# Diagonal attention: the turned query rows stand once, half of the heads in each row group, in place of all heads in both

## The chip, the cores and the metric

The kernel runs on one core of a Trainium2 chip. The metric is device time in microseconds, the median of the runs shown.

## The reference, cut to what matters

Four blocks follow one another on a residual of 2 x 2048 tokens of 128 channels: a hybrid block (state space, time crystal, wavelet attention, mixture of experts), an FFN-like attention, the diagonal attention, and the FFN-like attention again. The change touches the third only:

```python
Q = (X_embed @ W_q + b_q) * scale      # K likewise, V without scale
Q, K, V = (t.reshape(n, heads, l, d) for t in (Q, K, V))   # heads 16, d 8
scores = jnp.einsum('neax,nebx->neab', Q, K)
A = jax.nn.softmax(scores, axis=2)     # over the queries a
diag = jnp.diagonal(A, axis1=2, axis2=3)
out = (diag[..., None] * V).reshape(n, l, hid)
return out @ W_o + b_o
```

The reshape has no transposition, so a "head" e of the reference is a block of 128 tokens, and its 2048 rows are 128 tokens times 16 slices of 8 channels. The kernel calls the slices heads. For each tile of 128 tokens it needs, for every key (128 tokens x 16 slices), the maximum and the sum of exponentials over all 2048 queries of the same tile. The order of the queries does not matter for either.

## The kernel before, in words

`phase_F` handles 32 tiles, one after another. For each, the projections are split into three bfloat16 parts, and the products of parts that matter stand as 64 rows (8 terms x 8 channels) per head: POOL spreads them token by token into `d_q_rows` and `d_k_rows` (L2471, L2478). TensorE turns them (L2289), and the copies into `d_qT` and `d_kT` (L2366 on VectorE, L2426 on ScalarE) leave 64 rows for each head, once in partitions 0 to 63 and once in 64 to 127, the two row groups of TensorE. There are four groups of 16 transposes for a tile: group 0 and 1 are the queries of heads 0 to 7 and 8 to 15, group 2 and 3 the keys. In each, all eight heads are turned into both row groups.

A tile has 32 steps, two for each key head: step n takes key head n // 2 and the query half n % 2. Its score is two matmuls side by side, one in each row group (L2304), into two of six PSUM banks; VectorE takes the maximum of the 1024 columns (L2372), ScalarE the exponentials with their sum (L2434, whose accumulator is read by an instruction of its own). The six banks are a ring of three steps: score n waits for the exponential of n - 3.

The order of the side work is written out by hand with generators. `beside` runs, after each of the 32 scores of tile t, one piece of the preparation of tile t + 1 and one piece of the closing of tile t - 1, on each of TensorE, VectorE and ScalarE. TensorE projects the next tile after score 0 (L2277), turns the output of the last tile after score 10 and multiplies it by the output weights after score 12 (L2312, L2316), and turns rows from score 14 on. VectorE copies group 0 after its reduction 16, ScalarE the groups 1, 2 and 3 after its exponentials 18, 20 and 22. POOL does the spreading and small arithmetic in one line: close tile t - 1, prepare tile t + 1. SyncE has only the loads ahead of the stage.

All side outputs of TensorE share the two remaining banks. The list `side` gives their order (projection, turned output, output, rows 0 to 3), and `pe_side` lets a unit wait until the one two places before it has been read: rows 2 for VectorE's copy of rows 0, rows 3 for ScalarE's copy of rows 1. In TensorE's order the wait for the spread query rows stands at step 14, that for the key rows ahead of group 2, at step 18. The stage's first tile is prepared with nothing beside it.

Lines that the steps touch: L2274 to L2294 `pe_prep`, L2246 `pe_side`, L2296 `pe_score`, L2319 `beside`, L2343 the wait for the last copy ahead of score 0, L2349 `dve_prep`, L2416 `act_prep`, L2429 `act_score`, and the wait on `turned` in `pool_prep`. The same two-row-group matmul stands in the FFN-like attention at L1872: `k2[half, w, h, f, :]` streams from the same columns of both halves.

Of the kernel before, what the change touches and what calls it, by code (L numbers as in the profile page):

```python
# [11 lines left out]
P = 128  # L12
D = 128
BANK = 512
# [85 lines left out]
def build(nc, a, out, shape, phases=("M", "T", "C", "D", "E", "F", "E2")):  # L100
# [5 lines left out]
    with ctx:  # L106
# [16 lines left out]
        def sb(stack, name, shp, dt=F32):  # L123
            return stack.enter_context(nc.sbuf_tensor(name, shp, dt))
# [2054 lines left out]
        def phase_F():  # L2179
# [7 lines left out]
            with ExitStack() as st:  # L2187
# [7 lines left out]
                part = sb(st, "d_parts", [P, 3, 2 * HID], BF16)  # L2195
                uq = sb(st, "d_q_rows", [P, 2, NH, len(TERMS), HD], BF16)
                uk = sb(st, "d_k_rows", [P, 2, NH, len(TERMS), HD], BF16)
                qT = sb(st, "d_qT", [2 * ROWS, 2, NH * P], BF16)
                kT = sb(st, "d_kT", [2 * ROWS, 2, NH * P], BF16)
                dg = sb(st, "d_diag", [P, 3, NH])  # L2200
                dj = sb(st, "d_diag_terms", [P, HID])
# [13 lines left out]
                biased = signal("diag_biased", tl)  # L2215
                q_spread = signal("diag_q_spread", tl)
                k_spread = signal("diag_k_spread", tl)
                turned = signal("diag_rows_turned", [(t, k) for t in tl for k in range(4)])
                row_dve = signal("diag_rows_dve", tl)
                row_act = signal("diag_rows_act", [(t, k) for t in tl for k in range(1, 4)])  # L2220
                scored = signal("diag_scored", range(R * STEPS))
                maxed = signal("diag_max", range(R * STEPS))
                summed = signal("diag_exp", range(R * STEPS))
# [12 lines left out]
                for t in range(-1, R + 1):  # L2236
                    if t + 1 < R:
                        side.append(("qkv", t + 1))
                    if 0 <= t - 1 < R:
                        side += [("turn", t - 1), ("out", t - 1)]  # L2240
                    if t + 1 < R:
                        side += [("rows", t + 1, k) for k in range(4)]
                side_at = {u: n for n, u in enumerate(side)}
                side_bank = lambda *u: side_at[u] % 2

# [26 lines left out]
                    leave(SP)  # L2272

                def pe_prep(t):  # L2274
                    b, i, s = t // NT, t % NT, t % 2
                    bk = pe_side("qkv", t)
                    T.matmul(bank(bk)[:, 0:3 * HID], chans[:, b, PAD + i * P:PAD + (i + 1) * P], w[:, :],  # L2277
                             start=True, stop=True).then_inc(*projected.up(t))
                    for _ in range(14):
                        yield  # L2280
                    T.wait_ge(*q_spread(t))
                    for k in range(4):
                        u = uk if k >= 2 else uq
                        if k == 2:
                            T.wait_ge(*k_spread(t))
                        rows = bank(pe_side("rows", t, k)).bitcast(BF16)
                        for q in range(8):
                            for r in range(2):
                                last = T.transpose(rows[ROWS * r:ROWS * r + ROWS, q * P:(q + 1) * P],  # L2289
                                                   u[:, s, 8 * (k % 2) + q].rearrange("p n x -> p (n x)"), identb[:, :])  # L2290
                            if q == 7:
                                last.then_inc(*turned.up(t, k))
                            if q % 3 == 2:
                                yield  # L2294

                def pe_score(t, n):  # L2296
                    s, jb, hf = t % 2, n // 2, n % 2
                    at = t * STEPS + n
                    if at >= 3:
                        T.wait_ge(*summed(at - 3))  # L2300
                    for jj in range(2):
                        c = 2 * hf + jj
                        half = slice(ROWS * jj, ROWS * jj + ROWS)
                        last = T.matmul(bank(2 + 2 * (at % 3) + jj), kT[half, s, jb * P:(jb + 1) * P], qT[half, s, c * BANK:(c + 1) * BANK],  # L2304
                                        start=True, stop=True)
                    last.then_inc(*scored.up(at))

# [22 lines left out]
                def pe():  # L2330
                    enter(T)
                    for b in range(NB):
                        T.wait_ge(*ln_out("F", b))
                        for g in range(4):
                            pe_turn_group("F", b, g, 4 * b + g, norm)
                    leave(T)
                    enter(T)
                    for _ in pe_prep(0):
                        pass

                    def score(t, n):
                        if n == 0:
                            T.wait_ge(*row_act(t, 3))  # L2343
                            T.wait_ge(*row_dve(t))
                        pe_score(t, n)
                    beside(pe_prep, pe_close, score)
                    leave(T)

                def dve_prep(t):  # L2349
                    s = t % 2  # L2350
                    bk = side_bank("qkv", t)
                    yield
                    V.wait_ge(*projected(t))
                    if t >= 1:
                        V.wait_ge(*k_spread(t - 1))
                    if t >= 3:
                        V.wait_ge(*closed(t - 3))
                    V.tensor_tensor(qf[:, s, :], bank(bk)[:, 0:2 * HID], bias[:, 0:2, :].rearrange("p n h -> p (n h)"), ALU.add)
                    V.tensor_tensor(vf[:, t % 3, :], bank(bk)[:, 2 * HID:3 * HID], bias[:, 2, :], ALU.add).then_inc(*biased.up(t))
                    for _ in range(15):  # L2360
                        yield
                    V.wait_ge(*turned(t, 0))
                    if t >= 2:
                        V.wait_ge(*scored((t - 1) * STEPS - 1))
                    rows = bank(side_bank("rows", t, 0)).bitcast(BF16)
                    V.tensor_copy(qT[:, s, 0:8 * P], rows).then_inc(*row_dve.up(t))  # L2366
                    yield

                def dve_score(t, n):
# [45 lines left out]

                def act_prep(t):  # L2416
                    s = t % 2
                    for k in range(1, 4):
                        for _ in range(18 if k == 1 else 2):
                            yield  # L2420
                        A.wait_ge(*turned(t, k))
                        if t >= 2:
                            A.wait_ge(*scored((t - 1) * STEPS - 1))
                        dst = kT if k >= 2 else qT
                        rows = bank(side_bank("rows", t, k)).bitcast(BF16)
                        A.copy(dst[:, s, (k % 2) * 8 * P:(k % 2 + 1) * 8 * P], rows).then_inc(*row_act.up(t, k))  # L2426
                    yield

                def act_score(t, n):  # L2429
# [29 lines left out]
                def pool_prep(t):  # L2459
                    s = t % 2  # L2460
                    heads = lambda x: x.rearrange("p (h o x) -> p h o x", o=1, x=HD)
                    G.wait_ge(*biased(t))
                    gstep(G.tensor_copy(part[:, 0, :], qf[:, s, :]))
                    gstep(G.tensor_tensor(rest[:, :], qf[:, s, :], part[:, 0, :], ALU.subtract))
                    gstep(G.tensor_copy(part[:, 1, :], rest[:, :]))
                    gstep(G.tensor_tensor(part[:, 2, :], rest[:, :], part[:, 1, :], ALU.subtract))
                    if t >= 2:
                        G.wait_ge(*turned(t - 2, 3))
                    for g in range(3):
                        rows = uq[:, s, :, of_q[g], :]  # L2470
                        last = G.tensor_copy(rows, wide(heads(part[:, g, 0:HID]), 2, rows.shape[2]))  # L2471
                        if g < 2:
                            gstep(last)
                    last.then_inc(*q_spread.up(t))
                    G.wait_ge(*q_spread(t))
                    for g in range(3):
                        rows = uk[:, s, :, of_k[g], :]
                        last = G.tensor_copy(rows, wide(heads(part[:, g, HID:2 * HID]), 2, rows.shape[2]))  # L2478
                        if g < 2:
                            gstep(last)  # L2480
                    last.then_inc(*k_spread.up(t))
                    G.wait_ge(*k_spread(t))
                    gstep(G.tensor_tensor(dj[:, :], qf[:, s, 0:HID], qf[:, s, HID:2 * HID], ALU.mult))
                    d4 = dj[:, :].rearrange("p (h x) -> p h x", x=HD)
                    gstep(G.tensor_tensor(d4[:, :, 0:4], d4[:, :, 0:4], d4[:, :, 4:8], ALU.add))
                    gstep(G.tensor_tensor(d4[:, :, 0:2], d4[:, :, 0:2], d4[:, :, 2:4], ALU.add))
                    gstep(G.tensor_tensor(dg[:, t % 3, :], d4[:, :, 0], d4[:, :, 1], ALU.add))
# [70 lines left out]
```

## Time and profile before

| | |
|---|---|
| median of 3 runs | 4824.35 us (4823.6 to 4824.75) |
| the profiled execution, its own time | 4827.53 us |
| its span | 4826.2 us |
| granted TensorE clock, mean | 0.801 |
| busy share of the span | TensorE 78%, VectorE 72%, ScalarE 61%, POOL 17% |
| the diagonal attention's tiles | 2693.4 us to about 4020 us of the span |

The span is counted from the first to the last instruction. In the page's chain of work that ended last, the reduction L2372 is the largest line with 11% and the exponential L2434 has 4%. Busy shares over the span average stages with different limits, so the stretches of the one stage are read below.

### The profile page before, as it was taken

What the parts mean: (1) busy time and instruction counts of PE and PEld (TensorE: products, weight loads), DVE (VectorE), ACT (ScalarE), POOL (GpSimd) and SP (SyncE); (2) the same over time, 40 slices, a digit from 0 to 9 for tenths busy, and PEclk for the clock granted to TensorE, in tenths of its full rate; (3) what the DMA queues carried; (4) which work ended last, traced back from release to release, by engine and by line L of the source; (5) the groups of instructions that cost most, each with busy time, mean ns of one, the idle gap of its engine ahead of it and who ended that gap; (6) DMA issues with size and microseconds to landing.
All of it is one profiled execution on the core that took longest, in us unless ns stands there. A gap on an engine that the chain in (4) does not pass through costs nothing.

```text
span 4826.2 us, 78862 instructions
## 1 busy us (share of the span) xinstructions
PE 3784.1 (78%) x31382; PEld 2009.6 (42%) x31382; DVE 3457.4 (72%) x5239; ACT 2956.7 (61%) x4913; POOL 838.6 (17%) x1094
## 2 busy tenths in 40 slices
PE   6888558858869996899999566666666664899998
PEld 4666333222234442567666211111111111567666
DVE  6888666476451003778787899999999996778787
ACT  3444126626623333566665699999999995566665
POOL 2444210000036762000000111111111110000000
PEclk8999759969979998999999555555555556999999
DMA  1000000000022210000000000000000000000000
GB/s 42 1 1 1 1 3 1 1 0 1 1 72 36 44 26 17 8 15 2 11 2 5 2 1 1 1 1 1 1 1 1 1 1 18 8 15 2 11 2 19
DMA packets 49884, 45.20 MB, mean 9 GB/s; under 512 B 21203, under 2 KB 34910, under 8 KB 49502
## 3 DMA queue, kind: packets, MB, share of 16 engines
q1 hardware_dynamic: 49518, 40.16, 4.0%
q8 instruction: 250, 4.10, 0.4%
q14 instruction: 116, 0.95, 0.1%
HBM read 29.52 MB, written 2.23 MB: 7 GB/s over the span
## 4 chain that ended last, share of the span: by engine, by line
PE 47%; DVE 29%; issue 11%; ACT 10%; POOL 2%; DMA 1%; SPq 1%; DVEq 0%; ACTq 0%; POOLq 0%
DVE d_negmax L2372 11%; PE psum L1872 7%; PE psum L1901 6%; PE psum L1887 5%; DVE f_m_E L2017 5%; PE psum L1507 5%; PE psum L1530 4%; ACT d_junk L2434 4%; PE psum L1124 2%; PE psum L1113 2%; PE psum L1098 2%; ACT wl_p L1345 2%; DVE f_pT_E L2036 1%; DVE wl_negmax L1250 1%; PE psum L498 1%
## 5 line engine op out<-in xcount | busy, mean ns | idle before, releaser
L2372 DVE TENSOR_REDUCE d_negmax<-psum 128x1 f32<-128x1024 f32 x1024 | 1184.6, 1215 | 101.4 <-PE psum L2304 101.4
L2434 ACT ACTIVATE d_junk<-psum,d_negmax 128x1024 bf16<-128x1024 f32 x1024 | 1137.8, 1128 | 75.7 <-DVE d_negmax L2372 68.0
L2304 PE MATMUL psum<-d_qT,d_kT 64*128 64x512 bf16 x2048 | 605.5, 600 | 440.6 <-ACT d_junk L2434 424.2
L2123 ACT ACTIVATE hidden<-psum,f_nm_E 128x1024 f32<-128x1024 f32 x512 | 566.5, 1113 | 141.7 <-DVE f_nm_E L2020 141.5
L2017 DVE TENSOR_REDUCE f_m_E<-psum 128x1 f32<-128x1024 f32 x512 | 602.3, 1218 | 47.7 <-PE psum L1872 47.5
L1872 PE MATMUL psum<-f_k_E,f_q_swapped_E 64*128 64x512 f32 x1024 | 526.9, 624 | 6.6 <-ACT hidden L2123 6.6
L1872 PE MATMUL psum<-f_k_E,f_q_E 64*128 64x512 f32 x1024 | 526.9, 624 | 2.8 <-DMA f_q_swapped_E<-f_q_E 1.4
L1901 PE MATMUL psum<-f_pT_E,f_v_E 128*64 128x128 f32 x8192 | 503.7, 276 | 2.5 <-DVE residual L2047 2.5
L2130 ACT COPY f_pT_E<-psum 128x512 f32<-128x512 f32 x512 | 300.1, 586 | 319.8 <-PE psum L1887 319.7
L2036 DVE COPY f_pT_E<-psum 128x512 f32<-128x512 f32 x512 | 351.7, 687 | 157.4 <-PE psum L1887 146.9
L2304 PEld LDWEIGHTS psum<-d_qT,d_kT 64*128 64x128 bf16 x2048 | 106.0, 101 | 857.9 <-ACT d_junk L2434 805.5
L1901 PEld LDWEIGHTS psum<-f_pT_E,f_v_E 128*64 128x64 f32 x8192 | 442.5, 137 | 20.1 <-ACT f_pT_E L2130 2.8
L1887 PEld LDWEIGHTS psum<-ident,hidden 64*128 64x128 f32 x8192 | 317.4, 140 | 234.8 <-issue 185.3
L1664 POOL TENSOR_TENSOR moe_h<-moe_h,moe_gates_on_all 128x512 f32<-128x512 f32 x256 | 322.8, 1294 | 494.2 <-DMA moe_gates_on_all<-moe_gate_spill 364.6
L1250 DVE TENSOR_REDUCE wl_negmax<-psum 128x1 f32<-128x1024 f32 x256 | 305.5, 1222 | 142.4 <-PE psum L1098 138.4
L1887 PE MATMUL psum<-ident,hidden 64*128 64x64 f32 x8192 | 358.6, 227 | 47.8 <-DVE f_pT_E L2036 44.8
L1649 ACT ACTIVATE moe_h<-psum,moe_b 128x512 f32<-128x512 f32 x256 | 175.4, 687 | 271.8 <-PE psum L1530 271.8
L1345 ACT ACTIVATE wl_p<-psum 128x1024 f32<-128x1024 f32 x256 | 253.2, 1026 | 110.8 <-PE psum L1113 110.4
L1507 PE MATMUL psum<-moe_h,moe_w 128*128 128x512 f32 x512 | 232.2, 597 | 8.9 <-POOL moe_h L1664 8.9
L1530 PE MATMUL psum<-normed_channels,moe_w 128*128 128x512 f32 x512 | 235.4, 604 | 0.0
L1594 DVE COPY moe_yT<-psum 128x512 f32<-128x512 f32 x8 | 5.5, 692 | 312.3 <-PE psum L1507 312.3
L2434 ACT ACTIVATION_READ_ACCUMULATOR d_junk<-psum,d_negmax 128x1 f32 x1024 | 216.6, 212 | 0.0
(313 smaller groups left out, 5246.5 us busy)
## 6 DMA issues: line engine op xcount, KB each, us to landing
moe_gates_on_all<-moe_gate_spill SPq DMA_DIRECT2D x8, 2048.0 KB, 15.8
f_q_swapped_E<-f_q_E SPq DMA_DIRECT2D x64, 128.0 KB, 2.4
moe_w<-in_moe_w SPq DMA_DIRECT2D x8, 256.0 KB, 4.0
out<-residual SPq DMA_DIRECT2D x1, 2048.0 KB, 8.7
residual<-in_hidden_states SPq DMA_DIRECT2D x2, 768.0 KB, 7.4
residual<-in_hidden_states SPq DMA_DIRECT2D x2, 256.0 KB, 3.4
m_taps<-in_m_conv SPq DMA_DIRECT2D x4, 128.0 KB
level_sums<-in_c_sums SPq DMA_DIRECT2D x1, 512.0 KB
```

The source lines that it names most:

```text
L1250: V.tensor_reduce(negm[:, i, h:h + 1], two(slot(*step)), X, ALU.max, negate=True).then_inc(*maxed.up(b, h, i))
L1507: last = T.matmul(acc, w2[:, e * FT + f, :], hbuf[:, n % 2, f, :], start=False, stop=(e == E_ - 1 and f == FT - 1))
L1530: T.matmul(bank(f), w1[:, e, f * P:(f + 1) * P], chans[:, b, PAD + g * BANK:PAD + (g + 1) * BANK], start=True, stop=True).then_inc(*made.u ...
L1872: last = T.matmul(bank(2 * f + jj), (q if jj == h else q_sw)[half, w, qs], k2[half, w, h, f, :], start=True, stop=True)
L1887: last = T.transpose(bank(4 + r)[:, q * 64:(q + 1) * 64], pb[half, u % 2, kt * P:(kt + 1) * P], ident[half, half])
L1901: last = T.matmul(bank(6)[64 * h:64 * h + 64, 0:P], vt[:, n % 2, kt, h, :], pT[:, (2 * t + h) % 4, kt, :], start=(kt == 0), stop=(kt == NT ...
L2017: last = V.tensor_reduce(m2[:, u % 4, f:f + 1], two(2 * f), X, ALU.max)
L2036: V.tensor_copy(pT[:, u % 4, 8 * g:8 * g + 8, 64:P], bank(5).rearrange("p (q n) -> p q n", n=64)).then_inc(*pT_dve.up(u, g))
L2123: A.activation(pb[:, u % 2, f * 2 * BANK:(f + 1) * 2 * BANK], two(2 * f), ACT.Exp, bias=nm[:, u % 4:u % 4 + 1], scale=SC, accum_out=rs[:, ...
L2304: last = T.matmul(bank(2 + 2 * (at % 3) + jj), kT[half, s, jb * P:(jb + 1) * P], qT[half, s, c * BANK:(c + 1) * BANK], start=True, stop=True)
L2372: V.tensor_reduce(mh[:, t % 2, n // 2, n % 2:n % 2 + 1], two(2 + 2 * (at % 3)), X, ALU.max, negate=True).then_inc(*maxed.up(at))
L2434: A.activation(junk[:, at % 3, :], two(2 + 2 * (at % 3)), ACT.Exp, bias=mh[:, t % 2, n // 2, n % 2:n % 2 + 1], accum_out=sh[:, t % 2, n // ...
```

## The change

The query rows are turned in one group in place of two. That group puts heads 0 to 7 into the first row group and heads 8 to 15 into the second. `d_qT` has half the columns. A step's two matmuls now take the same columns of `d_qT`, which are different heads in the two halves. The keys stay twice and are groups 1 and 2 now, copied by ScalarE after its exponentials 18 and 20.

```diff
--- before.py
+++ after.py
@@ -2195,7 +2195,7 @@
                 part = sb(st, "d_parts", [P, 3, 2 * HID], BF16)
                 uq = sb(st, "d_q_rows", [P, 2, NH, len(TERMS), HD], BF16)
                 uk = sb(st, "d_k_rows", [P, 2, NH, len(TERMS), HD], BF16)
-                qT = sb(st, "d_qT", [2 * ROWS, 2, NH * P], BF16)
+                qT = sb(st, "d_qT", [2 * ROWS, 2, NH * P // 2], BF16)
                 kT = sb(st, "d_kT", [2 * ROWS, 2, NH * P], BF16)
                 dg = sb(st, "d_diag", [P, 3, NH])
                 dj = sb(st, "d_diag_terms", [P, HID])
@@ -2215,9 +2215,9 @@
                 biased = signal("diag_biased", tl)
                 q_spread = signal("diag_q_spread", tl)
                 k_spread = signal("diag_k_spread", tl)
-                turned = signal("diag_rows_turned", [(t, k) for t in tl for k in range(4)])
+                turned = signal("diag_rows_turned", [(t, k) for t in tl for k in range(3)])
                 row_dve = signal("diag_rows_dve", tl)
-                row_act = signal("diag_rows_act", [(t, k) for t in tl for k in range(1, 4)])
+                row_act = signal("diag_rows_act", [(t, k) for t in tl for k in range(1, 3)])
                 scored = signal("diag_scored", range(R * STEPS))
                 maxed = signal("diag_max", range(R * STEPS))
                 summed = signal("diag_exp", range(R * STEPS))
@@ -2239,7 +2239,7 @@
                     if 0 <= t - 1 < R:
                         side += [("turn", t - 1), ("out", t - 1)]
                     if t + 1 < R:
-                        side += [("rows", t + 1, k) for k in range(4)]
+                        side += [("rows", t + 1, k) for k in range(3)]
                 side_at = {u: n for n, u in enumerate(side)}
                 side_bank = lambda *u: side_at[u] % 2
 
@@ -2272,6 +2272,7 @@
                     leave(SP)
 
                 def pe_prep(t):
                     b, i, s = t // NT, t % NT, t % 2
                     bk = pe_side("qkv", t)
                     T.matmul(bank(bk)[:, 0:3 * HID], chans[:, b, PAD + i * P:PAD + (i + 1) * P], w[:, :],
@@ -2279,15 +2280,16 @@
                     for _ in range(14):
                         yield
                     T.wait_ge(*q_spread(t))
-                    for k in range(4):
-                        u = uk if k >= 2 else uq
-                        if k == 2:
+                    for k in range(3):
+                        u = uk if k else uq
+                        if k == 1:
                             T.wait_ge(*k_spread(t))
                         rows = bank(pe_side("rows", t, k)).bitcast(BF16)
                         for q in range(8):
                             for r in range(2):
+                                eighth = 8 * (k - 1 if k else r) + q
                                 last = T.transpose(rows[ROWS * r:ROWS * r + ROWS, q * P:(q + 1) * P],
-                                                   u[:, s, 8 * (k % 2) + q].rearrange("p n x -> p (n x)"), identb[:, :])
+                                                   u[:, s, eighth].rearrange("p n x -> p (n x)"), identb[:, :])
                             if q == 7:
                                 last.then_inc(*turned.up(t, k))
                             if q % 3 == 2:
@@ -2299,9 +2301,8 @@
                     if at >= 3:
                         T.wait_ge(*summed(at - 3))
                     for jj in range(2):
-                        c = 2 * hf + jj
                         half = slice(ROWS * jj, ROWS * jj + ROWS)
-                        last = T.matmul(bank(2 + 2 * (at % 3) + jj), kT[half, s, jb * P:(jb + 1) * P], qT[half, s, c * BANK:(c + 1) * BANK],
+                        last = T.matmul(bank(2 + 2 * (at % 3) + jj), kT[half, s, jb * P:(jb + 1) * P], qT[half, s, hf * BANK:(hf + 1) * BANK],
                                         start=True, stop=True)
                     last.then_inc(*scored.up(at))
 
@@ -2340,7 +2341,7 @@
 
                     def score(t, n):
                         if n == 0:
-                            T.wait_ge(*row_act(t, 3))
+                            T.wait_ge(*row_act(t, 2))
                             T.wait_ge(*row_dve(t))
                         pe_score(t, n)
                     beside(pe_prep, pe_close, score)
@@ -2363,7 +2364,7 @@
                     if t >= 2:
                         V.wait_ge(*scored((t - 1) * STEPS - 1))
                     rows = bank(side_bank("rows", t, 0)).bitcast(BF16)
-                    V.tensor_copy(qT[:, s, 0:8 * P], rows).then_inc(*row_dve.up(t))
+                    V.tensor_copy(qT[:, s, :], rows).then_inc(*row_dve.up(t))
                     yield
 
                 def dve_score(t, n):
@@ -2415,15 +2416,14 @@
 
                 def act_prep(t):
                     s = t % 2
-                    for k in range(1, 4):
+                    for k in range(1, 3):
                         for _ in range(18 if k == 1 else 2):
                             yield
                         A.wait_ge(*turned(t, k))
                         if t >= 2:
                             A.wait_ge(*scored((t - 1) * STEPS - 1))
-                        dst = kT if k >= 2 else qT
                         rows = bank(side_bank("rows", t, k)).bitcast(BF16)
-                        A.copy(dst[:, s, (k % 2) * 8 * P:(k % 2 + 1) * 8 * P], rows).then_inc(*row_act.up(t, k))
+                        A.copy(kT[:, s, (k - 1) * 8 * P:k * 8 * P], rows).then_inc(*row_act.up(t, k))
                     yield
 
                 def act_score(t, n):
@@ -2465,7 +2465,7 @@
                     gstep(G.tensor_copy(part[:, 1, :], rest[:, :]))
                     gstep(G.tensor_tensor(part[:, 2, :], rest[:, :], part[:, 1, :], ALU.subtract))
                     if t >= 2:
-                        G.wait_ge(*turned(t - 2, 3))
+                        G.wait_ge(*turned(t - 2, 2))
                     for g in range(3):
                         rows = uq[:, s, :, of_q[g], :]
                         last = G.tensor_copy(rows, wide(heads(part[:, g, 0:HID]), 2, rows.shape[2]))
```

## Rows read from the trace of the kernel before

**Rows 1.** Busy time of two tiles: us, then PE, PEld, DVE, ACT, POOL; PEclk, DMA

```profile
2970.10:3011.61 41.51, 26.00 (x136) 7.63 (x138) 38.37 (x39) 39.08 (x70) 7.97 (x21) 0.54 0.00 1
3011.61:3053.12 41.51, 26.36 (x137) 7.64 (x139) 38.38 (x40) 39.10 (x70) 7.98 (x21) 0.50 0.00 1
```

**Rows 2.** Groups of instructions of the whole stage: busy us, mean ns | idle before

```profile
L2372 DVE TENSOR_REDUCE d_negmax<-psum 128x1 f32<-128x1024 f32 x1024 | 1184.6, 1215 | 101.4 <-PE psum L2304 101.4
L2434 ACT ACTIVATE d_junk<-psum,d_negmax 128x1024 bf16<-128x1024 f32 x1024 | 1137.8, 1128 | 75.7 <-DVE d_negmax L2372 68.0
```

**Rows 3.** VectorE's order of time over one tile: start us, us, what

```profile
3000.62 1.22 DVE L2372 TENSOR_REDUCE d_negmax<-psum 128x1 f32<-128x1024 f32 x1 [0.30 <-PE psum L2304]
...
3005.95 4.61 DVE L2372 TENSOR_REDUCE d_negmax<-psum 128x1 f32<-128x1024 f32 x4
3011.61 3.49 DVE L2372 TENSOR_REDUCE d_negmax<-psum 128x1 f32<-128x1024 f32 x3 [1.05 <-PE psum L2304]
3015.36 2.36 DVE L2372 TENSOR_REDUCE d_negmax<-psum 128x1 f32<-128x1024 f32 x2 [0.27 <-PE psum L2304]
3018.47 8.01 DVE L2372 TENSOR_REDUCE d_negmax<-psum 128x1 f32<-128x1024 f32 x7 [0.75 <-PE psum L2304]
3027.25 1.23 DVE L2372 TENSOR_REDUCE d_negmax<-psum 128x1 f32<-128x1024 f32 x1 [0.77 <-PE psum L2304]
```

**Rows 4.** ScalarE's order of time, from the end of exponential 18

```profile
3009.35 0.19 ACT L2434 ACTIVATION_READ_ACCUMULATOR d_junk<-psum,d_negmax 128x1 f32 x1
3009.44 1.00 ACT L2426 COPY d_qT<-psum 128x1024 bf16<-128x1024 bf16 x1
3010.33 1.13 ACT L2434 ACTIVATE d_junk<-psum,d_negmax 128x1024 bf16<-128x1024 f32 x1
3011.34 0.21 ACT L2434 ACTIVATION_READ_ACCUMULATOR d_junk<-psum,d_negmax 128x1 f32 x1
...
3012.52 1.03 ACT L2426 COPY d_kT<-psum 128x1024 bf16<-128x1024 bf16 x1
3013.41 1.15 ACT L2434 ACTIVATE d_junk<-psum,d_negmax 128x1024 bf16<-128x1024 f32 x1
3014.42 0.23 ACT L2434 ACTIVATION_READ_ACCUMULATOR d_junk<-psum,d_negmax 128x1 f32 x1
...
3016.50 1.18 ACT L2434 ACTIVATE d_junk<-psum,d_negmax 128x1024 bf16<-128x1024 f32 x1
3017.51 0.26 ACT L2434 ACTIVATION_READ_ACCUMULATOR d_junk<-psum,d_negmax 128x1 f32 x1
```

**Rows 5.** TensorE's order of time at score 21

```profile
3010.49 0.53 PE L2289 MATMUL psum<-ident_bf,d_k_rows 128*64 128x128 bf16 x6 [1.07 <-ACT d_qT L2426]
3010.96 0.61 PE L2304 MATMUL psum<-d_qT,d_kT 64*128 64x512 bf16 x2
```

**Rows 6.** Groups of the stage: the transposes of key and query rows

```profile
L2289 PE MATMUL psum<-ident_bf,d_k_rows 128*64 128x128 bf16 x992 | 90.1, 307 | 35.1 <-ACT d_qT L2426 35.1
L2289 PE MATMUL psum<-ident_bf,d_q_rows 128*64 128x128 bf16 x992 | 85.7, 314 | 0.0
```

**Rows 7.** Order of time: TensorE's step 16; POOL's key rows one tile later

```profile
3003.68 0.75 PE L2289 MATMUL psum<-ident_bf,d_q_rows 128*64 128x128 bf16 x10
...
3040.91 1.55 POOL L2478 COPY d_k_rows<-d_parts 128x384 bf16<-128x384 bf16 x3
```

**Rows 8.** Order of time: the first preparation

```profile
2688.12 1.54 POOL L2478 COPY d_k_rows<-d_parts 128x384 bf16<-128x384 bf16 x3
...
2692.32 1.01 ACT L2426 COPY d_kT<-psum 128x1024 bf16<-128x1024 bf16 x1
...
2693.39 0.61 PE L2304 MATMUL psum<-d_qT,d_kT 64*128 64x512 bf16 x2 [1.11 <-ACT d_kT L2426]
```

**Rows 9.** Groups of a stretch of the second FFN attention, its score matmuls

```profile
L1872 PE MATMUL psum<-f_k_E,f_q_swapped_E 64*128 64x512 f32 x416 | 213.0, 623 | 0.0
L1872 PE MATMUL psum<-f_k_E,f_q_E 64*128 64x512 f32 x416 | 212.9, 622 | 0.0
```

## The prediction

> **What bounds the kernel now.** I looked first at the busy time by stretch. One tile of the diagonal attention takes 41.51 us, ScalarE is busy 39.08 and VectorE 38.37 of it; TensorE has room, and its granted clock is 0.50 to 0.54, so nearly all of the stage runs at 1.2 GHz [rows 1]. Then the groups of the stage: VectorE idles 101.4 us, all of it waiting for score matmuls, and ScalarE 68.0 us, waiting for VectorE's maxima [rows 2]. Neither is full, so a cycle holds them. Score n may not start before the exponential of n-3 has freed its two banks, and a reduction needs its score, an exponential its reduction. Third, VectorE's order of time shows where the idle time of a tile sits: back-to-back reductions start every 1.13 us ((8.01 - 1.22) / 6), and one tile has waits of 1.05, 0.27, 0.75, 0.77 and 0.30 us [rows 3]. The three beginning with 1.05, together 2.07, lie at scores 21, 24 and 26, behind the three ScalarE copies of turned rows at steps 18, 20 and 22 [rows 4]. Last, TensorE's order of time: score 21 starts at 3010.96 only because transposes of the fourth group stand ahead of it, and they waited 1.07 us for ScalarE's copy to free a side bank [rows 5]; over the stage it is 35.1 us in 992 / 32 = 31 tiles, all those that prepare a successor [rows 6].
>
> **The change part by part, per prepared tile.**
> Removed on TensorE: 16 of 64 transposes, 0.53 us per six, so about 1.4 us of busy time [rows 5]. TensorE waits for others between scores, so by itself this is worth nothing; the wait in front of them counts below. The first group now turns different heads in its two row groups instead of one head twice; query and key transposes cost 314 and 307 ns now [rows 6], so I take no difference.
> Removed on ScalarE: the copy at step 18 or, seen from the end, the third one. Between exponentials it takes 3010.33 - 3009.44 = 0.89 us of ScalarE's order [rows 4]. VectorE's copy of the first group keeps its shape and place.
> Scores: same count, shapes and banks, only the query columns differ. Maximum and sum run over 1024 other queries of the same 2048; cost nothing.
> Moved: key groups come two steps earlier in TensorE's order, and so does the wait for the spread key rows, from step 18 to step 16. Score 17, and with it VectorE and ScalarE, queue behind it. POOL ends those rows at 3040.91 + 1.55 - 41.51 = 3000.95 of the shown tile; step 16's transposes start at 3003.68 [rows 7]. The cover is 2.7 us; without it the excess would be paid in full. The second key group waits for VectorE's copy at step 18, as the third group does now, without idling. The next projection, the turn and the output find their banks free long before. No DMA moves.
>
> **The sum, by replaying the tile from reduction 17.** Three constants: pace 1.13 us; from the end of an accumulator read to the reduction three steps on, 0.70 us (3014.42 + 0.23 = 3014.65 to 3015.36; 3017.51 + 0.26 = 3017.77 to 3018.47); exponential slot 1.10 us, copy slot 0.89 [rows 3, 4]. Times from here are 3000 plus. Reductions 17 to 20 stay: 5.95, 7.08, 8.21, 9.34. Without the bank wait, 21 starts at the pace, 10.47 (the exponential of 18 ended at 9.54, plus 0.70 = 10.24). Exponentials 19 and 20 stay at 10.33 and 11.43, the last copy is at 12.52, 21 and 22 stay at 13.41 and 14.51, and 23 comes at 15.61 in place of 16.50. So reduction 22 waits for exponential 19: 11.34 + 0.21 + 0.70 = 12.25 (a wait of 0.65); 23 at 13.38; 24 waits for exponential 21: 15.35 (a wait of 0.84); 25 at 16.48; 26 at 17.61, with exponential 23 ended at 16.85 and so no wait. Before, 26 started at 18.47: **0.86 us saved**. ScalarE's own chain says the same, one slot of 0.89 less before exponential 26. From there VectorE runs at its pace, and the waits at the projection (0.77) and at the output (0.30) repeat, since what makes them stands in TensorE's own order. So 2.07 of idle time becomes about 1.2 to 1.5: of the 1.05 removed, most of what follows is late next because the ring has only three places.
>
> 31 tiles x 0.86 = 26.7 us. In the first preparation, where nothing covers it, the third copy and its transposes go, but the first key group must wait for POOL until 2688.12 + 1.54 = 2689.66. The bounds are zero (that wait eats it all) and one whole copy, 1.01, the one that ended just before the score at 2693.39 [rows 8]; I take the middle, 0.5, as neither end has a row for it. Sum 27.2. The profiled execution took 4827.53 with a span of 4826.2, and would take 4800.3; the median of the runs shown is 3.2 below it, 4824.35, which gives **4797.2 us**.
>
> Where no row decides, bounds. Per tile the gain lies between half of the above, 0.43 (the ring waits at 22 and 24 hand on more than I let them), and 1.05 (only the wait goes, nothing grows): 4810.5 to 4791.3. I take 0.86, since both the VectorE replay and ScalarE's chain give it.
>
> **Two rules weighed.** ScalarE is the busier engine by 0.71 us per tile [rows 1], and a rule that looked at occupancy alone would stop the gain there, where VectorE becomes the fuller: 31 x 0.71 + 0.5 = 22.5, or 4801.8. The Trainium skill, Perfetto Trace Analysis, Identifying the Most-Contended Engine, ranks engines in just that way and would have the fullest worked on first. The trace speaks against a floor there, since VectorE still idles 3.14 us per tile and is not full either way.
> A tile with clock 0.54 and one with 0.50 both take 41.51 us [rows 1], so a lower clock here costs nothing that a row shows, down to the 1.2 GHz at which nearly all of it runs already. The Trainium skill, TensorE: Matmul & The Clock Gate, HAM oscillation, says that TensorE left idle gets the lower clock, which speaks against taking transposes away; by it the sum stays as it is.
>
> **The rivals.**
> A, the copies become hidden: with two in place of three the ring absorbs them, all of 2.07 goes, and VectorE sets the time: 4824.35 - 31 x 2.07 - 0.5 = 4759.7. For it: VectorE would still be busy 38.4 of 39.4. Against: each copy delays the score three steps on by 0.89, and the ring's slack is 3 x 1.13 less one round of about 3.15 (0.70 + 1.22 + 1.21 + handover), some 0.24 us. 5%.
> B, no measurable change: the saved slot comes back in front of reductions 22, 24 and the projection, or the heads' new order adds a wait that balances it; under 0.3 us per tile remains, 4815 to 4824. For it: waits in this loop are handed on. Against: from 3009.35 to 3017.51 each operation of ScalarE starts as the one before it ends, so a slot taken out there must show [rows 4]. Also here: the text does not do what it says and a fourth group is still turned; the diff's loops leave no place for one. 7%.
> C, slower: the two score matmuls of a pair now read the same query columns in both row groups, where before they read different ones. If these reads had to take turns, the second 512 columns would come behind the first. 512 columns at 1.2 GHz are 0.43 us beside the 0.61 of a pair now [rows 1, 5]; four waits per tile grow by that, 1.72, and a round of 3.58 exceeds three paces by 0.19, 32 / 3 x 0.19 = 2.0. Less 0.86, that is 2.9 per tile, 32 x 2.9 = 92: 4916. It decides from about 0.22 us on (four waits alone then eat 0.86). Against: in the FFN attention two 64-row matmuls read their moving operand, the key tile, at equal columns in both halves, and both groups show the same busy time, 213 us, side by side [rows 9]. 3%.
>
> **How the numbers follow.** The forecast with its bounds has 85%, A 5%, B 7%, C 3%. About 0.2%, 9.6 us, is what a measurement of this kernel can tell from no change; the weak end of the forecast, 4810.5, still lies beyond it, B mostly does not. The range 4790 to 4810 takes in the bounds and leaves out A, B and C, 15%, and a little at the edges. Faster by over 0.2%: 0.90; within: 0.07; slower: 0.03.
>
> **What would show it.** In VectorE's order of time the period should be 40.6 to 40.7 us; no wait at score 21; waits of about 0.6 at 22 and 0.8 at 24; none at 26; 0.77 and 0.30 unchanged. ScalarE should show 64 copies in place of 96 and the wait of key transposes for a ScalarE copy should be gone. POOL's key rows should end over 2 us before the first key transposes. Wrong would be: score matmuls longer than 0.61 a pair (C), a projection or output wait that has grown (B), or a tile near 39.5 (A).

## The result and the profile after

The changed kernel takes 4795.72 us, the median of 4 runs (4794.66 to 4796.81), against 4823.98 us of the kernel before in the same comparison. The ratio is 0.9943, with a 95% interval of 0.9925 to 0.9960: faster by 0.6%. The forecast was 4797.2 in 4790 to 4810. The profiled execution has a span of 4795.5 us, 30.7 less than before. One of the ten executions of run e2 below took 8661.88 us, for a cause that nothing on record shows, and is left out of its ratio; the median of that run is 4822.6 with or without it.

First the two tiles that answer to [rows 1]. Columns as there: the stretch and its us, busy time of PE, PEld, DVE, ACT and POOL, then PEclk.

```profile
2975.71:3016.36 40.65, 23.82 (x119) 6.68 (x117) 38.28 (x39) 38.24 (x69) 7.93 (x21) 0.58 0.00 1
3016.36:3057.01 40.65, 24.91 (x119) 6.87 (x117) 38.28 (x40) 38.23 (x69) 7.94 (x21) 0.54 0.00 1
```

A tile takes 40.65 us in place of 41.51. ScalarE's busy time fell by 0.85 and VectorE's by 0.1, and the two engines are now equally full, 38.2 and 38.3 us. Neither is full: VectorE still waits 2.37 us in each tile for score matmuls. The granted clock of these two tiles is 0.58 and 0.54, not lower than before.

VectorE's order of time over one tile, which answers to [rows 3]:

```profile
2990.59 1.23 DVE L2373 TENSOR_REDUCE d_negmax<-psum 128x1 f32<-128x1024 f32 x1 [0.30 <-PE psum L2305]
...
2995.33 0.68 DVE L2367 COPY d_qT<-psum 128x1024 bf16<-128x1024 bf16 x1
2995.93 5.74 DVE L2373 TENSOR_REDUCE d_negmax<-psum 128x1 f32<-128x1024 f32 x5
3002.22 2.36 DVE L2373 TENSOR_REDUCE d_negmax<-psum 128x1 f32<-128x1024 f32 x2 [0.56 <-PE psum L2305]
3005.33 10.28 DVE L2373 TENSOR_REDUCE d_negmax<-psum 128x1 f32<-128x1024 f32 x9 [0.75 <-PE psum L2305]
3016.36 1.23 DVE L2373 TENSOR_REDUCE d_negmax<-psum 128x1 f32<-128x1024 f32 x1 [0.76 <-PE psum L2305]
```

The reader should compare starts. Reductions 17 to 21 now run as one piece of five (they were four and a stop of 1.05). Reduction 22 starts at 3002.22, 24 at 3005.33, and from 24 on nine run without a stop. The waits of 0.76 (the next tile's projection) and 0.30 (the output matmul) are where they were. The sum of waits in a tile went from 3.14 to 0.56 + 0.75 + 0.76 + 0.30 = 2.37. That is 0.77 of the 0.86; the rest is in the overlap at each stop (a reduction lasts 1.22 us but follows the last one after 1.13, and a stop hides 0.09 of its length in the end of the instruction before it, so three stops lose more than two).

The groups of the stage, in answer to [rows 2, 6]:

```profile
L2373 DVE TENSOR_REDUCE d_negmax<-psum 128x1 f32<-128x1024 f32 x1024 | 1181.8, 1216 | 77.0 <-PE psum L2305 77.0
...
L2291 PE MATMUL psum<-ident_bf,d_k_rows 128*64 128x128 bf16 x1024 | 86.5, 311 | 0.5 <-POOL d_k_rows L2478 0.5
L2426 ACT COPY d_kT<-psum 128x1024 bf16<-128x1024 bf16 x64 | 64.8, 1014 | 12.0 <-PE psum L2291 12.0
```

ScalarE makes 64 key copies, where it made 96 copies of rows; no ScalarE copy of query rows is left. The key transposes no longer wait for ScalarE, where 35.1 us stood; the 0.5 us for POOL are those of the first preparation, where nothing covers it. VectorE's idle time for scores is 77.0 us, against 101.4.

The first preparation, in answer to [rows 8]:

```profile
2684.64 1.54 POOL L2478 COPY d_k_rows<-d_parts 128x384 bf16<-128x384 bf16 x3
...
2687.41 1.93 ACT L2426 COPY d_kT<-psum 128x1024 bf16<-128x1024 bf16 x2 [12.03 <-PE psum L2291]
...
2689.39 0.61 PE L2305 MATMUL psum<-d_qT,d_kT 64*128 64x512 bf16 x2 [1.25 <-ACT d_kT L2426]
```

From POOL's key rows to the first score it is 2689.39 - 2684.64 = 4.75 us, before 2693.39 - 2688.12 = 5.27: 0.52 saved.

**The account of the span.** From the first score to the end of the last tile's maxima (the VectorE minimum after it) the stage took 4018.49 - 2693.39 = 1325.10 us before and 3987.79 - 2689.39 = 1298.40 now: 26.70 less. The preparation gives 0.52. What follows the stage is 807.71 us in both. The remaining 3.5 us lie ahead of the stage, in code that did not change. They come from the wavelet attention: its reductions L1250 start from 685.3 to 1270.9 us before and from 687.3 to 1267.5 now. They begin 2.0 us later and lie 5.4 us closer together, which is 3.4 us gained. Its stretch in busy times and clock, before and then now:

```profile
687.00:1271.00 584.00, 468.51 (x2663) 167.03 (x2660) 376.37 (x464) 321.72 (x349) 8.90 (x7) 0.85 0.00 1
```

```profile
687.00:1268.00 581.00, 461.74 (x2667) 162.82 (x2665) 378.31 (x465) 322.10 (x349) 8.89 (x7) 0.87 0.00 1
```

The mean clock is 0.85 against 0.87 in the same code. I take this for scatter of the two profiled executions and not for the change: in the eight runs below, none of which changes this code, the same reductions take between 581.9 and 583.7 us from first to last, against 585.6 before and 580.2 after. The medians differ by 28.3 us, nearer to the 27.2 that the stage and its preparation give.

### The profile page after: what moved, and what is told of

It reads as the page before. It is cut to its first block, busy times and chain, and to the rows that moved or that the text cites. A ratio compares the mean times of both kernels' runs of the same rounds, so it can differ in the third digit from the quotient of the medians.

```text
span 4795.5 us, 77776 instructions
## 1 busy us (share of the span) xinstructions
PE 3740.9 (78%) x30870; PEld 1980.5 (41%) x30870; DVE 3451.2 (72%) x5239; ACT 2927.5 (61%) x4881; POOL 837.1 (17%) x1094
## 4 chain that ended last, share of the span: by engine, by line
PE 47%; DVE 29%; issue 11%; ACT 9%; POOL 2%; DMA 1%; SPq 1%; DVEq 0%; POOLq 0%; ACTq 0%
DVE d_negmax L2373 11%; PE psum L1872 7%; PE psum L1901 6%; PE psum L1887 5%; DVE f_m_E L2017 5%; PE psum L1507 5%; PE psum L1530 4%; ACT d_junk L2434 4%; PE psum L1124 2%; PE psum L1113 2%; ACT wl_p L1345 2%; DVE wl_negmax L1250 2%; PE psum L1098 2%; DVE f_pT_E L2036 1%; PE psum L498 1%
## 5 line engine op out<-in xcount | busy, mean ns | idle before, releaser
L1250 DVE TENSOR_REDUCE wl_negmax<-psum 128x1 f32<-128x1024 f32 x256 | 305.3, 1222 | 138.3 <-PE psum L1098 134.2
```

Source lines behind the costliest of these rows:

```text
L1250: V.tensor_reduce(negm[:, i, h:h + 1], two(slot(*step)), X, ALU.max, negate=True).then_inc(*maxed.up(b, h, i))
```

## The experiments

The expectations speak of a ring theory. It is the rule by which the prediction replayed the tile: the six banks hold three scores, and score n waits for exponential n - 3, so a wait on the way to a score counts only if it ends later than that exponential does. By this, what cost time was the third copy's slot in ScalarE's line, and the wait for the side bank was only the place where it was seen. Its main rival: the bank wait of 1.05 us, the largest idle gap of VectorE, was the cost itself. The stage is compared by the time from the start of the first reduction to the start of the last, in each profiled execution; it is free of what happens ahead of the stage. "Tile" is the median time from one tile's VectorE minimum to the next one's. The kernel before was measured again beside e1 to e4 (median 4822.54 us) and beside e5 to e8 (4823.70), and the ratios below are to these; e1, e2 and e6 have ten executions, the others four.

| run | median us | first to last reduction | tile |
|---|---|---|---|
| before | 4823.98 | 1322.0 | 41.51 |
| after | 4795.72 | 1295.3 | 40.65 |
| e1, three copies, no bank wait | 4822.94 | 1321.5 | 41.49 |
| e2, third slot back | 4822.63 | 1321.5 | 41.49 |
| e3, bank wait back | 4793.69 | 1294.1 | 40.64 |
| e4, other columns | 4799.94 | 1295.2 | 40.65 |
| e5, copy beside copy | 4775.37 | 1275.6 | 40.01 |
| e6, key rows late | 4830.33 | 1323.5 | 41.59 |
| e7, key rows a little late | 4799.08 | 1295.3 | 40.65 |
| e8, projection beside copy | 4754.14 | 1251.9 | 39.27 |

### e1: the kernel before without the bank wait ahead of score 21

```diff
+                        if k == 3:
+                            yield
...
-                        for _ in range(18 if k == 1 else 2):
+                        for _ in range({1: 18, 2: 2, 3: 3}[k]):
```

> The kernel before with its fourth group of transposes one step later on TensorE (behind score 21) and its third ScalarE copy one step later: the wait for the side bank no longer stands ahead of score 21, but all three copies stay. Ring theory (a copy's slot on ScalarE is what costs, the bank wait is only where it shows): VectorE's wait at score 21 goes, waits of about 0.6 at 22 and 0.8 at 24 come, and one of about 0.7 stays near 26 or 27; tile 41.5 us, time within 3 us of before, 4821 to 4827. Rival (the bank wait itself cost 1.05 us per tile): 31 x 1.05 = 33 us less, 4791.

The ratio to before is 1.000 (0.999 to 1.001). VectorE's order of time:

```profile
2962.11 5.74 DVE L2374 TENSOR_REDUCE d_negmax<-psum 128x1 f32<-128x1024 f32 x5
2968.41 2.35 DVE L2374 TENSOR_REDUCE d_negmax<-psum 128x1 f32<-128x1024 f32 x2 [0.56 <-PE psum L2306]
2971.51 3.49 DVE L2374 TENSOR_REDUCE d_negmax<-psum 128x1 f32<-128x1024 f32 x3 [0.74 <-PE psum L2306]
2975.71 6.88 DVE L2374 TENSOR_REDUCE d_negmax<-psum 128x1 f32<-128x1024 f32 x6 [0.71 <-PE psum L2306]
```

The stop of 1.05 us at reduction 21 is gone: five run in one piece. In its place there are stops of 0.56, 0.74 and 0.71 at reductions 22, 24 and 27, one for each copy of ScalarE's. Taking the most visible wait away gave nothing. This is the rival's clearest failure; it stood to win 33 us. The edit also moves the third copy one step, from exponential 22 to 23, so e1 alone does not separate the wait from the copy's place; e3 returns the wait and moves no copy.

### e2: the changed kernel with a third ScalarE slot

```diff
+                spare = sb(st, "d_spare", [P, 8 * P], BF16)
...
-                        A.copy(kT[:, s, (k - 1) * 8 * P:k * 8 * P], rows).then_inc(*row_act.up(t, k))
+                        done = A.copy(kT[:, s, (k - 1) * 8 * P:k * 8 * P], rows)
+                        if k == 2:
+                            for _ in range(2):
+                                yield
+                            done = A.copy(spare[:, :], rows)
+                        done.then_inc(*row_act.up(t, k))
```

> The changed kernel with a third ScalarE copy after exponential 22, of the last group once more into a tile that nobody reads, so the slot is back and no transposes and no bank wait with it. Ring theory: VectorE waits again at about reduction 26, 0.86 us per tile, 31 x 0.86 = 27: 4822. Rival (the gain came from the bank wait or the transposes): no change, 4796.

The ratio to before is 1.0002 (0.9993 to 1.0012): the whole gain is given back by one ScalarE copy, without any transposes.

```profile
3000.91 5.74 DVE L2374 TENSOR_REDUCE d_negmax<-psum 128x1 f32<-128x1024 f32 x5
3007.21 2.35 DVE L2374 TENSOR_REDUCE d_negmax<-psum 128x1 f32<-128x1024 f32 x2 [0.56 <-PE psum L2306]
3010.31 2.35 DVE L2374 TENSOR_REDUCE d_negmax<-psum 128x1 f32<-128x1024 f32 x2 [0.75 <-PE psum L2306]
3013.41 8.01 DVE L2374 TENSOR_REDUCE d_negmax<-psum 128x1 f32<-128x1024 f32 x7 [0.75 <-PE psum L2306]
```

The copy stands ahead of exponential 23, and the third stop, 0.75 us, is back at reduction 26, whose score waits for that exponential. The rival, by which nothing would change from 4796, fails.

### e3: the changed kernel with the bank wait and the transposes back

```diff
-                    for k in range(3):
+                    for k in range(4):
...
+                        elif at[1] == 3:
+                            pass
...
-                                eighth = 8 * (k - 1 if k else r) + q
+                                eighth = 8 * (k - 1 if k in (1, 2) else r) + q
...
-                            if q == 7:
+                            if q == 7 and k < 3:
```

The list of side banks has four groups again; the fourth turns key rows a second time and is read by nobody.

> The changed kernel with a fourth group of 16 transposes that nobody copies, in its old place and behind its old wait for ScalarE's copy of the second group: TensorE's work and the bank wait are back ahead of score 21, ScalarE's third copy is not. Ring theory: score 21 comes 1.1 us late again, but the waits at 22 and 24 shrink by as much, because reduction 24 is held by exponential 21 at the same time anyway; tile 40.6 to 40.8 us, 4796 to 4800. Rival (the bank wait itself cost 1.05 us per tile): 31 x 1.05 = 33 more, 4829.

TensorE waits for ScalarE's copy just as before the change, 1.06 us, and then VectorE:

```profile
2999.71 0.53 PE L2293 MATMUL psum<-ident_bf,d_k_rows 128*64 128x128 bf16 x6 [1.06 <-ACT d_kT L2428]
```

```profile
2995.17 4.60 DVE L2375 TENSOR_REDUCE d_negmax<-psum 128x1 f32<-128x1024 f32 x4
3000.82 3.48 DVE L2375 TENSOR_REDUCE d_negmax<-psum 128x1 f32<-128x1024 f32 x3 [1.05 <-PE psum L2307]
3004.57 10.27 DVE L2375 TENSOR_REDUCE d_negmax<-psum 128x1 f32<-128x1024 f32 x9 [0.26 <-PE psum L2307]
```

VectorE stops 1.05 us at reduction 21, then 0.26 at 24, and the tile is that of the changed kernel, 40.64 us against 40.65. So 16 transposes per tile and a bank wait of 1 us on TensorE are free here, where the rival had 4829. Reduction 24 starts 9.40 us after reduction 17 in this run and in the changed kernel, since in both it is exponential 21 that holds it. The median, 4793.69, is even 2 us below the changed kernel's, of which the stage shows 1.2 (1294.1 against 1295.3); the two were not compared on the same runs and I make nothing of it.

### e4: the two row groups read different columns

```diff
-                        last = T.matmul(bank(2 + 2 * (at % 3) + jj), kT[half, s, jb * P:(jb + 1) * P], qT[half, s, hf * BANK:(hf + 1) * BANK],
+                        last = T.matmul(bank(2 + 2 * (at % 3) + jj), kT[half, s, jb * P:(jb + 1) * P], qT[half, s, (hf ^ jj) * BANK:((hf ^ jj) + 1) * BANK],
```

> The changed kernel with the two matmuls of a score reading different columns of the query rows (the second row group takes the other half of its heads), as the kernel before did. Theory: equal columns in both row groups cost nothing, so 4796 and a pair of 0.61 us. Rival (equal columns take turns in part): shorter score pairs and less than 4796, by 4 us for each 0.03 us per wait.

The stage takes 1295.2 us against 1295.3, and the scores' matmuls have a mean of 600 ns in both. Rival C is out: equal columns cost nothing. The median of 4799.94 is not in the stage: its four runs are 4794.72, 4796.22, 4803.67 and 4803.9, and in the profiled one the first score comes at 2696.2 us, 6.8 us later than in the changed kernel's.

### e5: ScalarE's first copy beside VectorE's copy

```diff
-                        for _ in range(18 if k == 1 else 2):
+                        for _ in range(16 if k == 1 else 4):
```

> The changed kernel with ScalarE's first key copy two steps earlier, right after exponential 16, where ScalarE idles 0.52 us while VectorE makes its own copy; the second copy stays after exponential 20. Ring theory: a copy costs only what it delays beyond the wait already there, so exponential 17 moves by 0.3 to 0.4 us and the wait of 0.56 at reduction 22 goes; tile 40.1 us, 31 x 0.55 = 17 less than the changed kernel, 4779. Rival (each ScalarE copy costs its 0.86 wherever it stands, since ScalarE is the fuller engine): 4796.

The ratio to before is 0.9906 (0.9889 to 0.9922). ScalarE first, then VectorE:

```profile
2989.56 0.19 ACT L2434 ACTIVATION_READ_ACCUMULATOR d_junk<-psum,d_negmax 128x1 f32 x1
2989.68 1.01 ACT L2426 COPY d_kT<-psum 128x1024 bf16<-128x1024 bf16 x1
2990.58 1.12 ACT L2434 ACTIVATE d_junk<-psum,d_negmax 128x1024 bf16<-128x1024 f32 x1
```

```profile
2989.03 8.08 DVE L2373 TENSOR_REDUCE d_negmax<-psum 128x1 f32<-128x1024 f32 x7
2997.79 10.27 DVE L2373 TENSOR_REDUCE d_negmax<-psum 128x1 f32<-128x1024 f32 x9 [0.68 <-PE psum L2305]
3008.82 1.23 DVE L2373 TENSOR_REDUCE d_negmax<-psum 128x1 f32<-128x1024 f32 x1 [0.76 <-PE psum L2305]
```

The copy starts as the accumulator read of exponential 16 ends, in the 0.52 us that ScalarE idled there anyway, and reductions 17 to 23 run as one piece. One stop of 0.68 stays. 19.7 us less than the changed kernel's stage, 0.64 per tile. Exponential 17 starts 1.55 us after reduction 17 (2990.58 - 2989.03), against 1.24 in the changed kernel (2997.17 - 2995.93): of the copy's slot of 0.89 only 0.31 delays it. The rival, a cost of 0.86 wherever the copy stands, had 4796 and fails. What the copy costs in its new place in all was not measured, since no run leaves it out; if it cost 0.86 in its old place, as the third copy did, about 0.2 is left.

### e6 and e7: how much cover the earlier wait for the key rows has

```diff
-                    for g in range(3):
+                    for n in range(12):
+                        g = n % 3
                         rows = uk[:, s, :, of_k[g], :]
```

e7 has 6 in place of 12.

> The changed kernel with POOL writing the key rows four times over, 9 copies of 0.51 us more, so they come 4.6 us later. In the changed kernel's trace they end 2.96 us before the first key transposes. Theory: these transposes wait about 1.6 us, score 17 starts as late, reduction 17 about 0.8 us late, and that is kept: tile 41.4 us, 31 x 0.8 = 25 more, 4821. Rival (a late side input is absorbed by the ring): below 4800.

> As the run before, but the key rows written twice, 3 copies more, 1.54 us later: inside the cover of 2.96 us. Theory: tile 40.65 us and 4796. Rival (POOL's line is already on the path): up to 31 x 1.54 = 48 more.

In e7 POOL's six copies take 3.15 us in place of 1.54, and the tile stays at 40.65 us: inside the cover. In e6 the twelve take 6.34, 4.8 us more, and the tile is 41.59:

```profile
2962.72 0.53 PE L2291 MATMUL psum<-ident_bf,d_k_rows 128*64 128x128 bf16 x6 [1.67 <-POOL d_k_rows L2479]
...
2963.83 2.35 DVE L2373 TENSOR_REDUCE d_negmax<-psum 128x1 f32<-128x1024 f32 x2 [0.86 <-PE psum L2305]
```

The key transposes wait 1.67 us for POOL and reduction 17 comes 0.86 us late by its idle time, 0.94 by the tile. So about half of the lateness arrives. In the changed kernel score 17 starts at 2994.44 and reduction 17, which also stands behind VectorE's copy, at 2995.93; from a score's start to its reduction it is 0.65 us where nothing else holds the reduction (3001.57 to 3002.22), so score 17 was 0.84 us early, and this is taken up first. In the stage that is 1323.5 - 1295.3 = 28.2 us, 0.91 per tile. The expectation of 25 was a little low. The median, 4830.33 in runs from 4826 to 4835, lies some 6 us above what the stage explains, and the cause of these 6 us stays open. So the moved wait is real and covered in the changed kernel. Past its cover, what makes reduction 17 late stays in the tile.

### e8: the projection behind score 23 as well

```diff
+                    if t + 1 < R:
+                        for _ in range(3):
+                            yield
+                        pe_project(t + 1)
...
+                    if t + 1 < R:
+                        for _ in range(8):
+                            yield
+                        dve_bias(t + 1)
```

`pe_project` and `dve_bias` hold the projection and the two bias additions, taken out of the preparations; the list of side banks has the projection behind the rows. ScalarE's copies are as in e5.

> As the run with ScalarE's first copy after exponential 16, and TensorE projects the tile after next behind score 23, where score 24 waits for the delay of ScalarE's second copy anyway, in place of behind score 0; VectorE adds the biases after reduction 24. Ring theory: the wait of 0.76 at reduction 1 goes, and 0.1 to 0.3 stays or comes at 24; tile 39.4 to 39.6 us, 4760 to 4765. Rival (waits add up wherever they stand): 40.1 us, 4779.

The ratio to before is 0.9859 (0.9843 to 0.9876), the best of all: 4754.14 against 4823.7 in the same comparison, 69.6 us less. Like e5 it leaves nothing of the computation out. TensorE, then VectorE:

```profile
2989.38 0.61 PE L2311 MATMUL psum<-d_qT,d_kT 64*128 64x512 bf16 x2 [0.49 <-ACT d_junk L2448]
2989.91 1.65 PE L2277 MATMUL psum<-d_w,normed_channels 128*128 128x384 f32 x2
2991.49 0.61 PE L2311 MATMUL psum<-d_qT,d_kT 64*128 64x512 bf16 x2
```

```profile
2983.26 8.09 DVE L2386 TENSOR_REDUCE d_negmax<-psum 128x1 f32<-128x1024 f32 x7
2992.14 1.23 DVE L2386 TENSOR_REDUCE d_negmax<-psum 128x1 f32<-128x1024 f32 x1 [0.79 <-PE psum L2311]
2993.28 0.41 DVE L2365 TENSOR_TENSOR d_qk<-psum,d_b 128x256 f32<-128x256 f32 x1
...
2993.81 10.26 DVE L2386 TENSOR_REDUCE d_negmax<-psum 128x1 f32<-128x1024 f32 x9
```

The projection (1.65 us) fills the time in which score 24 had to wait for exponential 21, and one stop of 0.79 stands where there were two, of 0.68 and 0.76. The reduction before the additions is number 24. The tile is 39.27 us, 0.74 less than e5. The rival, waits that add up wherever they stand, had 4779 and fails.

## Why the prediction was right

**The per-tile saving** was 0.86 and came out as 41.51 - 40.65 = 0.86. The replay named starts, and they can be laid on the trace: from reduction 17 to 22, 24 and 26 it had 6.30, 9.40 and 11.66 us. The trace has 3002.22 - 2995.93 = 6.29, 3005.33 - 2995.93 = 9.40, and with two paces more 11.66 (the rows show no single start for reduction 26, only that nine run without a stop). The waits that it gave as 0.65 and 0.84 read 0.56 and 0.75 in the rows; the replay measured them from the pace, the rows from the end of the instruction before, and 1.22 - 1.13 = 0.09 lies between the two ways.

**That most of the 1.05 us would be handed on** held, and e1 and e3 show why more strictly than the prediction had it: none of it was worth anything by itself. With three copies its removal gains 0 (e1), with two its return costs 0 (e3). The bound of 1.05 us per tile was therefore too generous. e2 shows that the slot is the whole of it: one more copy takes the stage from 1295.3 to 1321.5 us, against 1322.0 before.

**The first preparation**, 0.5 by halving the bounds, came out as 0.52; that was a lucky middle, not a reading. The sum of 27.2 us is what the stage and its preparation gave; the medians moved by 28.3, and that they moved no further off is luck as well, since the code ahead of the stage gave 3.5 us in the profiled executions.

**The cover of POOL's rows** was given as 2.7 us, from the start of step 16. The key transposes themselves begin at 2993.86, and POOL ends at 2989.36 + 1.54 = 2990.90, so 2.96 us; e6 and e7 lie on the two sides of it. What the prediction said beyond the cover, that "the excess would be paid in full", was wrong: in e6 the transposes wait 1.67 us and the tile grows by 0.94, because score 17 had 0.84 us to spare. The forecast did not use that sentence. TensorE's order at the place:

```profile
2993.86 0.53 PE L2291 MATMUL psum<-ident_bf,d_k_rows 128*64 128x128 bf16 x6
...
2996.77 0.39 PE L2305 MATMUL psum<-d_qT,d_kT 64*128 64x512 bf16 x2
...
2999.56 0.39 PE L2305 MATMUL psum<-d_qT,d_kT 64*128 64x512 bf16 x2 [0.51 <-ACT d_junk L2434]
3001.57 0.61 PE L2305 MATMUL psum<-d_qT,d_kT 64*128 64x512 bf16 x2 [1.62 <-ACT d_junk L2434]
```

**Columns in both row groups**, rival C: measured at nothing by e4. **No change**, B: the two waits outside the stretch, 0.76 and 0.30, did not grow. **All waits gone**, A: did not come, 0.56 and 0.75 stayed, because two copies still stand in ScalarE's line one after the other.

**The two rules.** A floor where VectorE becomes the fuller engine would have given 4801.8. The kernel went below that to 4795.72, and e8 to 4754.14, while VectorE's work was the same. By the rule of the Trainium skill (Perfetto Trace Analysis, Identifying the Most-Contended Engine) the fullest engine is the one to relieve; that was right about where the slot was worth something, but occupancy told nothing of the size. The rule of the Trainium skill on the clock (TensorE: Matmul & The Clock Gate, HAM oscillation), that idleness of TensorE lowers it, shows nothing here: the mean over the stage is 0.52 before and after. The rows at 2996.77 and 2999.56 above, 0.39 us a pair in place of 0.61, are at 2.4 GHz (granted clock 1.00 from 2996.7 to 3000.0), behind key transposes. They gain nothing either, since the scores after them wait for ScalarE: in the tile of e3 shown above scores 19 and 21 take 0.60 and 0.61 us, and reduction 24 follows reduction 17 after 9.40 us all the same.

## What to carry to other kernels

In a ring of few buffers between two nearly full engines, replay one period with three constants (the pace, the way round, the slot of the side work) before trusting a gap: the largest idle gap may be worth nothing and the work before it everything. Side work then costs by where it stands. Put the side instruction of one engine where another's already holds the ring, and two delays cost one; here two such moves, e5 and e8, gave 41.6 us, more than the 28.3 of the change itself.

## What was not expected

The edges of the kernel move more than a small effect does. The stage's own time was the same within 0.1 us in the changed kernel, e4 and e7. The time ahead of it differed by 3.5 us between before and after, and by 6.8 us between the changed kernel and e4, the first with clock 0.85 and 0.87 in the stretch shown. An effect of half a per cent in one stage is read better from the period of its tiles than from the median of four runs.

The projection could be hidden almost whole: 1.65 us of TensorE, for which VectorE had waited 0.76, now cost about 0.1 (0.79 against 0.68). That is within the 0.1 to 0.3 that was expected, and yet e8 came out 6 us below its range. Two parts of 0.09 us per tile explain it: e5, on which it builds, had a tile of 40.01 in place of 40.1, and a stop that goes takes with it the 0.09 us of overlap reckoned above, so the tile fell by 0.76 - 0.11 + 0.09 = 0.74. Over 31 tiles the two parts make 5.6 us.
